# Two operations of the expert weights' rounding moved to GpSimd, and the context's keys and values started earlier

## The chip, the cores and the metric

The kernel runs on one core of a Trainium2 chip. The metric is the device time of one execution in microseconds, as the median of the runs; lower is better.

## The reference

Eight blocks of a transformer, each added to `x` (8 x 128 x 256, f32). The change lies in the second block, a mixture of experts, and in a piece of the seventh block that is computed beside it:

```python
x = x + _L0_xattn_ref(_layernorm(x), ctx_2048, ctx_2048)
x = x + _L0_ffn_ref(_layernorm(x), L0_ffn_gate_w, L0_ffn_w13, L0_ffn_w2, ...)
...
def mxfp8_qdq(x):                      # blocks of 32 along the last axis
    amax = jnp.max(jnp.abs(xb), axis=-1, keepdims=True)
    exp = jnp.floor(jnp.log2(jnp.where(amax > 0, amax, 1.0)))
    scale = jnp.exp2(jnp.clip(exp - E4M3_MAX_POW2, -127.0, 127.0))
    q = jnp.clip(xb / scale, -E4M3_MAX, E4M3_MAX).astype(jnp.float8_e4m3fn)
    return (q.astype(x.dtype) * scale).reshape(shp)
...
scores = jax.nn.sigmoid(xf @ gate_w.T)        # 8 experts, the best 2 of scores + bias
xq = mxfp8_qdq(routed)                        # tokens times their score
w13q, w2q = mxfp8_qdq(w13), mxfp8_qdq(w2)     # the experts' weights
h = silu(xq @ w13q_1) * (xq @ w13q_3)
out = mxfp8_qdq(h) @ w2q + shared expert
...
k = (inputs_kv @ Wk)   # L3 attention: keys and values of the context,
v = (inputs_kv @ Wv)   # which depend on no earlier block
```

## The kernel before

The stages run one after the other, with a barrier of all engines between them. Each stage is a block of five programs, one for each engine, that meet by semaphores; each program is executed in the order in which it is written. The first stage (`stage_l0_xattn`) is the first attention, with nothing on SP. The second (`stage_l0_ffn`) is the expert block. Its order on the engines, up to the first up projection:

- **SP** issues the loads of the gate and the shared expert, then of `wk` and `wv` (L535, 2 MB each), then for each of 24 pairs of weight tiles (`PAIRS`, 16 of `w13` and 8 of `w2`) the rows `wrow` (L542, two buffers) and, three pairs behind, the stores of the finished keys and values (L548, L552).
- **GpSimd** makes masks `diag` (L580, identity times routing mask, two operations of 128 x 1024 for each sequence): four sequences at once, the other four later, as the masks are used up.
- **VectorE** normalises (L228 to L238), copies the transposed tokens (L593), routes (L600 to L615), finishes the shared expert (L623, L627), rounds the tokens of three sequences (`quantise_tokens`, L635 and `mx_round`), then rounds the weights, pair by pair (`prep`, `mx_round`). `mx_round` is eleven operations on a 128 x 512 tile: mask of the exponents (L207, `magic`), maximum of each block of 32 (L208), five small ones on 128 x 16 (L209 to L214), the scale operation (L215), the addition of a large number and its subtraction (L217, L218), which round to the grid, and the upper and the lower cap (L219, L221). `order.step` makes the engine wait for the operation's own end before the next.
- **TensorE** transposes the tokens (L738), makes the gate's logits (L745), the shared expert (L753, L761), turns the tokens of the first sequence (`turn_tokens`, L774) and then, for each pair, transposes the rounded weights into `psW` (L788) and makes the units of keys and values that belong to the pair (`unit`, L796 for keys, L801 for values: 64 units of two products of 128 x 512, 2 or 3 a pair). Behind the last unit come the up projections (L819) of the first sequence.
- **ScalarE** copies what TensorE made: `xm` (L694), `wT` (L701), `held` (L707).

A pair's semaphores are `row_loaded` (SP to VectorE), `wq_ready` (rounded; to TensorE, and to SP for the next load), `turned` and `wT_ready`.

## Time and profile before

| what | us |
|---|---|
| median of 3 runs | 1996.21 (1995.42 to 1996.57) |
| the profiled execution, its own time | 2003.36 |
| its span, first to last instruction | 2001.6 |
| TensorE busy | 1613.5 (81%) |
| VectorE busy | 1387.7 (69%) |
| ScalarE busy | 823.7 (41%) |
| GpSimd busy | 605.3 (30%) |

The span is what the trace covers; the execution's own time is 1.8 us longer. The expert block lies at 80.5 to 396 us. "PEclk" in the views is the clock that was granted to TensorE, as a share of 2.4 GHz. PE is TensorE, PEld its weight loads, DVE VectorE, ACT ScalarE, POOL GpSimd, SP the engine that only issues DMAs here.

### The profile page before, as it was taken

What the parts mean: (1) busy time and instruction counts of PE and PEld (TensorE: products, weight loads), DVE (VectorE), ACT (ScalarE), POOL (GpSimd) and SP (SyncE); (2) the same over time, 40 slices, a digit from 0 to 9 for tenths busy, and PEclk for the clock granted to TensorE, in tenths of its full rate; (3) what the DMA queues carried; (4) which work ended last, traced back from release to release, by engine and by line L of the source; (5) the groups of instructions that cost most, each with busy time, mean ns of one, the idle gap of its engine ahead of it and who ended that gap; (6) DMA issues with size and microseconds to landing.
All of it is one profiled execution on the core that took longest, in us unless ns stands there. A gap on an engine that the chain in (4) does not pass through costs nothing. (4 is left out here: it accounts for less than half of the span.)

```text
span 2001.6 us, 30042 instructions
## 1 busy us (share of the span) xinstructions
PE 1613.5 (81%) x9326; PEld 1135.7 (57%) x9326; DVE 1387.7 (69%) x3901; ACT 823.7 (41%) x2380; POOL 605.3 (30%) x739
## 2 busy tenths in 40 slices
PE   3559998879353788988889699999987999799883
PEld 2424434356122466666666488788774555688872
DVE  6679969678796688888888634676555333468875
ACT  1113444457332466666667433333331222244451
POOL 0020003067401777777777430111122000321000
PEclk7579999969665999999999899999997999899996
DMA  1305620010382900000000150000035222522200
GB/s 63 110 1 158 194 101 1 13 67 1 9 156 75 343 1 1 2 1 1 1 1 2 31 173 1 26 12 12 11 144 149 75 87 74 179 103 101 69 25 11
DMA packets 103590, 129.34 MB, mean 65 GB/s; under 512 B 14160, under 2 KB 89136, under 8 KB 99984
## 3 DMA queue, kind: packets, MB, share of 16 engines
q1 hardware_dynamic: 94448, 112.39, 17.7%
q0 software_dynamic: 8992, 15.08, 3.6%
q8 instruction: 78, 1.28, 0.3%
q14 instruction: 72, 0.59, 0.1%
HBM read 85.75 MB, written 46.94 MB: 66 GB/s over the span
## 5 line engine op out<-in xcount | busy, mean ns | idle before, releaser
L2326 PE MATMUL l2fa_psQ<-l2fa_xT,l2f_home 128*128 128x128 f32 x1024 | 124.9, 283 | 0.7 <-DMA l2f_home<-in_L2f_kvT 0.7
L2326 PEld LDWEIGHTS l2fa_psQ<-l2fa_xT,l2f_home 128*128 128x128 f32 x1024 | 121.8, 199 | 3.1 <-issue 1.6
L580 POOL TENSOR_TENSOR l0f_diag<-g_identb,l0f_mask 128x1024 bf16<-128x1024 bf16 x16 | 32.0, 2025 | 227.7 <-PE l0f_psA L836 208.8
L2817 ACT ACTIVATE l2x_probs<-l2x_psS,l2x_nmax 128x128 f32<-128x128 f32 x256 | 90.7, 371 | 10.2 <-DVE l2x_nmax L2731 10.0
L2601 POOL TENSOR_TENSOR l2x_probs<-l2x_probs,l2x_rtotal 128x512 f32<-128x512 f32 x64 | 66.8, 1043 | 90.2 <-DVE l2x_rtotal L2737 90.2
L3102 POOL TENSOR_TENSOR route_rrms<-route_vrms,g_minus_half 128x1 f32<-128x1 f32 x8 | 5.7, 707 | 270.6 <-DVE route_vrms L3124 270.6
L2612 POOL TENSOR_TENSOR l2x_vsm<-l2x_vraw,l2x_smooth_row 128x512 f32<-128x512 f32 x64 | 84.7, 1345 | 3.7 <-ACT l2x_vraw L2851 3.4
L3687 POOL DMA_INDIRECT routed_rows<-rows,route_slot_of x32 | 31.2, 975 | 175.7 <-DMA rows<-moe_yg 167.0
L3511 DVE COPY moe_xgT<-moe_psX 128x256 f32<-128x256 f32 x47 | 20.0, 425 | 91.1 <-PE moe_psX L3617 91.1
L2962 PEld LDWEIGHTS l2x_psS<-l2x_kT,l2x_qT 128*128 128x128 f32 x512 | 66.8, 192 | 22.3 <-issue 17.9
L1427 ACT ACTIVATE l2fa_probs<-l2fa_psS,l2fa_bias 128x128 f32<-128x128 f32 x128 | 45.2, 365 | 76.6 <-DVE l2fa_bias L1411 76.6
L1040 ACT ACTIVATE l1a_probs<-l1a_psS,l1a_nmax 128x256 f32<-128x256 f32 x128 | 58.9, 472 | 42.1 <-PE l1a_psT L1068 29.7
L819 PE MATMUL l0f_psH<-l0f_wT,l0f_xm 128*128 128x512 bf16 x256 | 68.0, 390 | 9.7 <-DVE l0f_h L660 9.0
L960 POOL TENSOR_TENSOR l1a_probs<-l1a_probs,l1a_rtotal 128x512 f32<-128x512 f32 x64 | 65.2, 1040 | 32.7 <-DVE l1a_rtotal L998 32.7
L2860 ACT COPY l2x_pT<-l2x_psT 128x512 f32<-128x512 f32 x64 | 37.5, 586 | 90.2 <-PE l2x_psT L2970 90.2
L3610 PE MATMUL moe_psG<-l2f_home,moe_xgT 128*128 x188 | 68.0, 484 | 5.1 <-issue 1.5
L2978 PE MATMUL l2x_psO<-l2x_pT,l2x_vsm 128*128 128x128 f32 x512 | 70.5, 283 | 0.0
L2363 PE MATMUL l2fa_psY<-l2fa_wo,l2fa_oT 128*128 128x256 f32 x256 | 62.9, 390 | 8.5 <-DVE l2fa_oT L2233 8.5
L2962 PE MATMUL l2x_psS<-l2x_kT,l2x_qT 128*128 128x128 f32 x512 | 67.8, 276 | 1.8 <-ACT l2x_probs L2817 1.7
L2363 PE MATMUL l3a_psY<-l2f_home,l3a_oT 128*128 128x256 f32 x256 | 62.9, 390 | 7.4 <-DVE l3a_oT L2233 7.1
L2326 PE MATMUL l3a_psQ<-l3a_xT,routed_wq 128*128 128x128 f32 x512 | 65.2, 282 | 2.9 <-ACT l3a_qT L2283 2.3
L2583 POOL TENSOR_TENSOR l2x_qrstd<-l2x_qve,g_minus_half 128x4 f32<-128x4 f32 x64 | 65.3, 1020 | 5.3
(571 smaller groups left out, 4690.2 us busy)
## 6 DMA issues: line engine op xcount, KB each, us to landing
rows<-l2x_zero SPq DMA_DIRECT2D x1, 18304.0 KB, 59.9
kT_ctx<-l0f_held SPq DMA_DIRECT2D x32, 256.0 KB, 3.5
v_ctx<-l0f_held SPq DMA_DIRECT2D x32, 256.0 KB, 3.7
l3a_kT<-kT_ctx SPq DMA_DIRECT2D x8, 1024.0 KB, 5.3
l3a_v<-v_ctx SPq DMA_DIRECT2D x8, 1024.0 KB, 5.6
l0f_wrow<-in_L_ffn_w SPq DMA_DIRECT2D x24, 256.0 KB, 3.0
moe_xg<-rows SPq DMA_DIRECT2D x47, 128.0 KB, 2.0
rows<-moe_yg SPq DMA_DIRECT2D x47, 128.0 KB, 1.7
```

The source lines that it names most:

```text
L819: last = nc.tensor.matmul(psH[:, k, :], xm[b % 2][:, k, c, e, :], wT[:, 2 * e:2 * e + 2, c, :], start=(e == 0 and c == 0), stop=(e == E0 - ...
L960: nc.gpsimd.tensor_tensor(probs[:, u, j, :, :], probs[:, u, j, :, :], rtotal[:, u, j, :].unsqueeze(2).to_broadcast([P, 2, D]), ALU.mult)\
L1040: last = nc.scalar.activation(probs[:, u, j, m, :], psS[2 * u + j][:, m, :], ACT.Exp, bias=nmax[:, u, j, m:m + 1], scale=1.0, accum_out=to ...
L2326: last = nc.tensor.matmul(psQ[bank][:, j, :], w[:, c, h * HD:(h + 1) * HD], xT[u][:, c, :], start=(c == 0), stop=(c == KC - 1))
L2363: last = nc.tensor.matmul(psY[:, :], oT[:, i % 2, j, :], wo[:, 4 * i + j, :], start=(i == 0 and j == 0), stop=(i == QUADS - 1 and j == 3))
L2583: ins = nc.gpsimd.tensor_tensor(qrstd[:, t % 2, :], qve[:, :], G.minus_half[:, 0:4], ALU.pow)
L2601: nc.gpsimd.tensor_tensor(probs[:, n % 2, :, :], probs[:, n % 2, :, :], rtotal[:, n % 2, :].unsqueeze(2).to_broadcast([P, 4, P]), ALU.mult)\
L2612: nc.gpsimd.tensor_tensor(vsm[:, j % 3, 4 * g:4 * g + 4, :].rearrange("p (g r) d -> p g r d", r=2), vraw[:, j % 2, 2 * g:2 * g + 2, :].uns ...
L2817: last = nc.scalar.activation(probs[:, n % 2, j, :], psS[:, j, :], ACT.Exp, bias=nmax[:, n % 2, j:j + 1], scale=1.0, accum_out=total[:, n ...
L2962: last = nc.tensor.matmul(psS[:, j, :], qT[:, n % 4, j, :], kT[:, n // 2 % 2, 2 * (n % 2) + j // 2, :], start=True, stop=True)
L2978: last = nc.tensor.matmul(psO[:, j, :], vsm[:, n // 2 % 3, 4 * (n % 2) + j, :], pT[:, n % 2, j, :], start=True, stop=True)
L3610: last = nc.tensor.matmul(psG[m % 3][:, 0:2 * I2], x, w, start=(c == 0), stop=(c == KC - 1))
```

## The change

1. `mx_round` is cut into `mx_level` (up to the scale operation), the two operations of the grid, and `mx_cap`. Tokens and hidden rows still go through all of it on VectorE. For the weights GpSimd does the addition and the subtraction (`snap`), and VectorE works on the level of pair n + 1 before the caps of pair n. There are two sets of `magic`, `sum`, `grid`, `top` and `bottom`, and three buffers of rows instead of two; a row is loaded again once the addition has read it.
2. The level of pair 0 is made ahead of the routing. The tokens of the first three sequences are rounded behind pairs 6, 12 and 18; the first sequence's are turned behind pair 20.
3. `wk` and `wv` are allocated outside the two stages and loaded by SP during the first attention.
4. TensorE makes five units before it transposes the tokens; the other 59 are spread over the pairs, and those of a pair come before its transposes instead of behind them.

The core of the diff:

```diff
+def mx_level(nc, order, m, src):
 
     dve = nc.vector
-    n, nb = m.n, m.nb
-    blocks = lambda ap: ap.rearrange("p (n k) -> p n k", k=BLOCK)
-    spread = lambda ap: ap.unsqueeze(2).to_broadcast([P, nb, BLOCK])
     order.mark(dve.tensor_scalar(m.magic[:, :].bitcast(I32), src.bitcast(I32), EXPONENT, None, ALU.bitwise_and))
-    order.step(dve.tensor_reduce(m.amax[:, :], blocks(src), AX.X, ALU.max, apply_absolute_value=True))
+    order.step(dve.tensor_reduce(m.amax[:, :], blocks_of(src), AX.X, ALU.max, apply_absolute_value=True))
     order.step(dve.tensor_scalar(m.exp[:, :].bitcast(I32), m.amax[:, :].bitcast(I32), EXPONENT, None,
                                  ALU.bitwise_and))
 
     dve.tensor_scalar(m.top[:, :], m.exp[:, :], 2.0 ** -119, 1.75, ALU.max, ALU.mult)
     dve.tensor_scalar(m.bottom[:, :], m.exp[:, :], 2.0 ** -119, -1.75, ALU.max, ALU.mult)
     order.step(dve.tensor_scalar(m.least[:, :], m.exp[:, :], 2.0 ** -119, GRID * 2.0 ** -14, ALU.max, ALU.mult))
-    order.step(dve.scalar_tensor_tensor(out=blocks(m.magic[:, :]), in0=blocks(m.magic[:, :]), scalar=GRID,
-                                        in1=spread(m.least[:, :]), op0=ALU.mult, op1=ALU.max))
-    order.step(dve.tensor_tensor(m.sum[:, :], src, m.magic[:, :], ALU.add))
-    order.step(dve.tensor_tensor(m.grid[:, :], m.sum[:, :], m.magic[:, :], ALU.subtract))
-    order.step(dve.tensor_tensor(blocks(m.grid[:, :]), blocks(m.grid[:, :]), spread(m.top[:, :]), ALU.min))
-
-    return dve.tensor_tensor(blocks(dst), blocks(m.grid[:, :]), spread(m.bottom[:, :]), ALU.max)
+    return dve.scalar_tensor_tensor(out=blocks_of(m.magic[:, :]), in0=blocks_of(m.magic[:, :]), scalar=GRID,
+                                    in1=spread_of(m, m.least[:, :]), op0=ALU.mult, op1=ALU.max)
...
+def mx_cap(nc, order, m, dst):
+    order.step(nc.vector.tensor_tensor(blocks_of(m.grid[:, :]), blocks_of(m.grid[:, :]), spread_of(m, m.top[:, :]), ALU.min))
+    return nc.vector.tensor_tensor(blocks_of(dst), blocks_of(m.grid[:, :]), spread_of(m, m.bottom[:, :]), ALU.max)
+
+
+def mx_round(nc, order, m, src, dst):
+    order.step(mx_level(nc, order, m, src))
+    order.step(nc.vector.tensor_tensor(m.sum[:, :], src, m.magic[:, :], ALU.add))
+    order.step(nc.vector.tensor_tensor(m.grid[:, :], m.sum[:, :], m.magic[:, :], ALU.subtract))
+    return mx_cap(nc, order, m, dst)
...
+class ContextWeights:
+
+
+    def __init__(self, nc, ctx, G):
+        T = Pool(nc, ctx, "l0k")
+        self.wk, self.wv = T.sb("wk", [P, KC, NH * HD]), T.sb("wv", [P, KC, NH * HD])
+        self.wk_loaded, self.wv_loaded = G.sem("wk_loaded"), G.sem("wv_loaded")
+
+    def load(self, sp, A):
+        sp.dma_start(self.wk[:, :, :], A["L3_xattn_Wk"].rearrange("(c p) o -> p c o", p=P)).then_inc(self.wk_loaded, 16)
+        sp.dma_start(self.wv[:, :, :], A["L3_xattn_Wv"].rearrange("(c p) o -> p c o", p=P)).then_inc(self.wv_loaded, 16)
+
+
+def stages_l0(nc, G, A):
+    with ExitStack() as ctx:
+        C = ContextWeights(nc, ctx, G)
+        stage_l0_xattn(nc, G, A, C)
+        stage_l0_ffn(nc, G, A, C)
...
+            @block.sync
+            def _(sp):
+                C.load(sp, A)
...
-        wrow = [T.sb(f"wrow{u}", [P, 2, D]) for u in range(2)]
+        ROWS = 3
+        wrow = [T.sb(f"wrow{u}", [P, 2, D]) for u in range(ROWS)]
         wq = [T.sb(f"wq{u}", [P, 2, D], BF16) for u in range(2)]
         wT = T.sb("wT", [P, PAIRS, KC, 2 * P], BF16)
         mx = Mx(T, "mx", 512)
+        wmx = [mx, Mx(T, "mx1", 512, mx)]
...
-        units_of = lambda n: range(n * UNITS // PAIRS, (n + 1) * UNITS // PAIRS)
-        PREP_STEPS = MX_STEPS
+        EARLY, LATE = 5, UNITS - 5
+        units_of = lambda n: range(EARLY + n * LATE // PAIRS, EARLY + (n + 1) * LATE // PAIRS)
+        TOKENS_AFTER, TURN_AFTER = {6: 0, 12: 1, 18: 2}, 20
...
-                for w, name in ((wk, "L3_xattn_Wk"), (wv, "L3_xattn_Wv")):
-                    sp.dma_start(w[:, :, :], A[name].rearrange("(c p) o -> p c o", p=P)).then_inc(kv_loaded, 16)
...
-                    wait(sp, wq_ready, n - 1)
+                    wait(sp, summed, n - ROWS + 1)
                     src = w13[n] if n < PAIRS13 else w2[n - PAIRS13]
-                    sp.dma_start(wrow[n % 2][:, :, :], src).then_inc(row_loaded[n % 2], 16)
+                    sp.dma_start(wrow[n % ROWS][:, :, :], src).then_inc(row_loaded[n % ROWS], 16)
 
                 def store(m):
                     sp.wait_ge(kv_copied, m + 1)
@@ -554,6 +591,9 @@
 
                 for n in range(PAIRS):
                     rows(n)
+                    if n == 3:
+                        for m in range(EARLY):
+                            store(m)
...
+                def snap(n):
+                    m = wmx[n % 2]
+                    pool.wait_ge(leveled, n + 1)
+                    nc.gpsimd.tensor_tensor(m.sum[:, :], wrow[n % ROWS][:, :, :].rearrange("p r d -> p (r d)"), m.magic[:, :],
+                                            ALU.add).then_inc(summed, 1)
+                    pool.wait_ge(summed, n + 1)
+                    wait(pool, wq_ready, n - 1)
+                    nc.gpsimd.tensor_tensor(m.grid[:, :], m.sum[:, :], m.magic[:, :], ALU.subtract).then_inc(snapped, 1)
+
                 for b in range(B):
+                    if b == 4:
+                        for n in range(PAIRS):
+                            snap(n)
...
+                prep = Order(dve, prep_order)
+
+                def level(n):
+                    dve.wait_ge(row_loaded[n % ROWS], 16 * (n // ROWS) + 16)
+                    mx_level(nc, prep, wmx[n % 2], wrow[n % ROWS][:, :, :].rearrange("p r d -> p (r d)")).then_inc(leveled, 1)
+
+                def cap(n):
+                    dve.wait_ge(snapped, n + 1)
+                    wait(dve, turned, n - 1)
+                    mx_cap(nc, prep, wmx[n % 2], wq[n % 2][:, :, :].rearrange("p r d -> p (r d)")).then_inc(wq_ready, 1)
+
+                level(0)
...
-                for b in range(3):
-                    quantise_tokens(b)
-
-                def prep(n, u):
-                    o = Order(dve, prep_order, n * PREP_STEPS)
-                    dve.wait_ge(row_loaded[u], 8 * (n - u) + 16)
-                    wait(dve, turned, n - 1)
-                    mx_round(nc, o, mx, wrow[u][:, :, :].rearrange("p r d -> p (r d)"),
-                             wq[u][:, :, :].rearrange("p r d -> p (r d)")).then_inc(wq_ready, 1)
-                    assert o.n == PREP_STEPS, o.n
-                in_pairs(dve, PAIRS, prep)
+                for n in range(PAIRS):
+                    if n + 1 < PAIRS:
+                        level(n + 1)
+                    cap(n)
+                    if n in TOKENS_AFTER:
+                        quantise_tokens(TOKENS_AFTER[n])
...
+                for m in range(EARLY):
+                    copy_unit(m)
...
-                copy_tokens(0)
...
                 for n in range(PAIRS):
-                    prep(n, n % 2)
                     for m in units_of(n):
                         copy_unit(m)
+                    prep(n, n % 2)
+                    if n == TURN_AFTER:
+                        copy_tokens(0)
...
+                pe.wait_ge(C.wk_loaded, 16)
+                for m in range(EARLY):
+                    unit(m)
+                pe.wait_ge(kv_copied, EARLY)
...
-                pe.wait_ge(shared_added, B)
-                for n in range(XM):
-                    turn_tokens(0, n)
-                pe.wait_ge(xm_ready, XM)
...
-                pe.wait_ge(kv_loaded, 32)
                 for n in range(PAIRS):
-                    prep(n, n % 2)
                     for m in units_of(n):
                         unit(m)
+                    prep(n, n % 2)
+                    if n == TURN_AFTER:
+                        pe.wait_ge(kv_copied, units_of(n).stop)
+                        for i in range(XM):
+                            turn_tokens(0, i)
+                        pe.wait_ge(xm_ready, XM)
```

How the order of VectorE's instructions changes for one pair (`prep_order`, `snapped`, `turned` and `row_loaded` are the semaphores waited for). Before, the second half of a pair and the start of the next:

```order
L215 SCALAR_TENSOR_TENSOR l0f_mx_magic<-l0f_mx_magic,l0f_mx_least 128x512 [waits l0f_prep_order]
L217 TENSOR_TENSOR l0f_mx_sum<-l0f_wrow,l0f_mx_magic 128x512 [waits l0f_prep_order]
L218 TENSOR_TENSOR l0f_mx_grid<-l0f_mx_sum,l0f_mx_magic 128x512 [waits l0f_prep_order]
L219 TENSOR_TENSOR l0f_mx_grid<-l0f_mx_grid,l0f_mx_top 128x512 [waits l0f_prep_order]
L221 TENSOR_TENSOR l0f_wq<-l0f_mx_grid,l0f_mx_bottom 128x512 [waits l0f_prep_order]
```

After, on VectorE:

```order
L219 SCALAR_TENSOR_TENSOR l0f_mx_magic<-l0f_mx_magic,l0f_mx_least 128x512 [waits l0f_prep_order]
L224 TENSOR_TENSOR l0f_mx_grid<-l0f_mx_grid,l0f_mx_top 128x512 [waits l0f_turned,l0f_snapped]
L225 TENSOR_TENSOR l0f_wq<-l0f_mx_grid,l0f_mx_bottom 128x512 [waits l0f_prep_order]
L211 TENSOR_SCALAR l0f_mx_magic<-l0f_wrow 128x512 [waits l0f_row_loaded2]
L212 TENSOR_REDUCE l0f_mx_amax<-l0f_wrow 128x16
L213 TENSOR_SCALAR l0f_mx_exp<-l0f_mx_amax 128x16 [waits l0f_prep_order]
```

and on GpSimd, behind the first masks, pairs 0 to 2 (`leveled` is set by the scale operation):

```order
L632 TENSOR_TENSOR l0f_diag<-g_identb,l0f_mask 128x1024 x7
L620 TENSOR_TENSOR l0f_mx_sum<-l0f_wrow,l0f_mx_magic 128x512 [waits l0f_leveled]
L624 TENSOR_TENSOR l0f_mx_grid<-l0f_mx_sum,l0f_mx_magic 128x512 [waits l0f_summed]
L620 TENSOR_TENSOR l0f_mx_sum<-l0f_wrow,l0f_mx_magic 128x512 [waits l0f_leveled]
L624 TENSOR_TENSOR l0f_mx_grid<-l0f_mx_sum,l0f_mx_magic 128x512 [waits l0f_summed]
L620 TENSOR_TENSOR l0f_mx_sum<-l0f_wrow,l0f_mx_magic 128x512 [waits l0f_leveled]
L624 TENSOR_TENSOR l0f_mx_grid<-l0f_mx_sum,l0f_mx_magic 128x512 [waits l0f_wq_ready,l0f_summed]
```

The addition and the subtraction have left VectorE's row of five; the scale operation's own end is no longer waited for by the operation behind it, and the caps are those of the pair before.

TensorE at the end of the loop, before (the last pair's transposes, its three units, the first up projection):

```order
L788 MATMUL l0f_psW<-g_identb,l0f_wq 128x128 x3
L801 MATMUL l0f_psA<-l0f_wv,g_ctxT 128x512 [waits l0f_kv_copied]
L801 MATMUL l0f_psA<-l0f_wv,g_ctxT 128x512
L801 MATMUL l0f_psA<-l0f_wv,g_ctxT 128x512 [waits l0f_kv_copied]
L801 MATMUL l0f_psA<-l0f_wv,g_ctxT 128x512
L801 MATMUL l0f_psA<-l0f_wv,g_ctxT 128x512 [waits l0f_kv_copied]
L801 MATMUL l0f_psA<-l0f_wv,g_ctxT 128x512
L819 MATMUL l0f_psH<-l0f_wT,l0f_xm 128x512 [waits l0f_xm_ready,l0f_wT_ready,l0f_kv_copied]
```

After, from the transposes of pair 20 on:

```order
L864 MATMUL l0f_psW<-g_identb,l0f_wq 128x128 x3
L855 MATMUL l0f_psA<-l0f_diag,l0f_zq 128x512 [waits l0f_diag_ready,l0f_zq_ready,l0f_kv_copied]
L855 MATMUL l0f_psA<-l0f_diag,l0f_zq 128x512 x3
L855 MATMUL l0f_psA<-l0f_diag,l0f_zq 128x512 [waits l0f_xm_ready] x4
L807 MATMUL l0f_psA<-l0k_wv,g_ctxT 128x512 [waits l0f_kv_copied,l0f_xm_ready]
```

The turning of the tokens stands between pair 20 and the eight units of pairs 21 to 23; the units of a pair stand ahead of its transposes, and nothing stands between the last transposes and the up projection (L885).

## Rows read from the trace of the kernel before

**Rows 1.** Busy us by stretch; behind the engines the granted clock, DMA share, GB/s.

```profile
core 0: us, PE busy (x) PEld busy (x) DVE busy (x) ACT busy (x) POOL busy (x), PEclk, DMA share, GB/s
80.00:88.00 8.00, 0.00 (x0) 0.00 (x0) 5.59 (x24) 0.00 (x0) 2.09 (x3) 0.50 0.57 146
100.00:104.00 4.00, 4.00 (x6) 1.86 (x7) 3.36 (x7) 1.51 (x2) 0.00 (x0) 0.50 0.03 12
104.00:110.00 6.00, 5.09 (x12) 1.91 (x10) 5.83 (x8) 1.19 (x2) 5.16 (x3) 1.00 0.00 0
131.00:154.00 23.00, 3.92 (x12) 1.24 (x13) 21.94 (x53) 4.01 (x8) 0.00 (x0) 0.58 0.00 0
170.00:271.50 101.50, 97.81 (x293) 43.59 (x292) 96.75 (x218) 41.38 (x73) 0.00 (x0) 1.00 0.62 189
```

**Rows 2.** Timeline, VectorE, a pair's ends: start us, duration us, engine, line, out<-in.

```profile
256.10 0.42 DVE L207 TENSOR_SCALAR l0f_mx_magic<-l0f_wrow 128x512 int32<-128x512 int32 x1
...
259.90 0.69 DVE L219 TENSOR_TENSOR l0f_mx_grid<-l0f_mx_grid,l0f_mx_top 128x512 bf16<-128x512 bf16 x1
260.62 0.69 DVE L221 TENSOR_TENSOR l0f_wq<-l0f_mx_grid,l0f_mx_bottom 128x512 bf16<-128x512 bf16 x1
261.23 0.42 DVE L207 TENSOR_SCALAR l0f_mx_magic<-l0f_wrow 128x512 int32<-128x512 int32 x1
```

**Rows 3.** Timeline, end of the loop; a unit is four records of L801.

```profile
262.20 3.65 PE L801 MATMUL l0f_psA<-l0f_wv,g_ctxT 128*128 128x512 f32 x8
...
266.74 5.37 PE L801 MATMUL l0f_psA<-l0f_wv,g_ctxT 128*128 128x512 f32 x12
...
270.89 0.69 DVE L221 TENSOR_TENSOR l0f_wq<-l0f_mx_grid,l0f_mx_bottom 128x512 bf16<-128x512 bf16 x1
...
272.17 5.37 PE L801 MATMUL l0f_psA<-l0f_wv,g_ctxT 128*128 128x512 f32 x12
...
278.21 0.60 PE L819 MATMUL l0f_psH<-l0f_wT,l0f_xm 128*128 128x512 bf16 x2 [0.68 <-ACT l0f_held L707]
```

**Rows 4.** Instructions of one line, GpSimd: duration ns min/median/max, first and last start.

```profile
L2601 POOL TENSOR_TENSOR l2x_probs<-l2x_probs,l2x_rtotal x64: 1030/1039/1097, 680.1 to 1132.8; 128x512 f32<-128x512 f32 x64
...
L2562 POOL TENSOR_TENSOR l2x_scaled<-l2x_xn,cw_in_row x16: 1256/1267/1276, 640.9 to 1013.7; 128x512 bf16<-128x512 f32 x16
```

**Rows 5.** Timeline, VectorE and GpSimd at the second and third later masks.

```profile
300.32 3.94 POOL L580 TENSOR_TENSOR l0f_diag<-g_identb,l0f_mask 128x1024 bf16<-128x1024 bf16 x2 [180.56 <-PE l0f_psA L836]
...
302.42 0.67 DVE L208 TENSOR_REDUCE l0f_mx_amax<-l0f_h 128x16 f32<-128x512 f32 x1
...
303.13 1.16 DVE L209 TENSOR_SCALAR l0f_mx_exp<-l0f_mx_amax 128x16 int32<-128x16 int32 x1
...
312.98 0.69 DVE L219 TENSOR_TENSOR l0f_mx_grid<-l0f_mx_grid,l0f_mx_top 128x512 bf16<-128x512 bf16 x1
...
313.07 4.66 POOL L580 TENSOR_TENSOR l0f_diag<-g_identb,l0f_mask 128x1024 bf16<-128x1024 bf16 x2 [8.81 <-PE l0f_psA L836]
...
313.71 2.27 DVE L221 TENSOR_TENSOR l0f_zq<-l0f_mx_grid,l0f_mx_bottom 128x512 bf16<-128x512 bf16 x1
```

**Rows 6.** Instructions of one line, start of the third stage, at 403 to 410.

```profile
L984 DVE TENSOR_SCALAR l1a_q<-g_x,l1a_mv,l1a_rstd x8: 396/481/4014, 403.3 to 409.7; 128x256 f32<-128x256 f32 x8
...
L952 POOL TENSOR_SCALAR l1a_ks<-g_ctx,l1a_parity x16: 478/479/504, 403.2 to 483.8; 128x256 f32<-128x256 f32 x16
```

**Rows 7.** Timeline, ahead of the loop: two token roundings' starts and the turned tokens' casts.

```profile
130.94 0.61 DVE L635 TENSOR_SCALAR l0f_z<-l0f_xf,l0f_wslot 128x256 f32<-128x256 f32 x2
...
136.72 0.61 DVE L635 TENSOR_SCALAR l0f_z<-l0f_xf,l0f_wslot 128x256 f32<-128x256 f32 x2
...
137.53 4.01 ACT L694 CAST l0f_xm<-l0f_psA 128x512 bf16<-128x512 f32 x8 [14.92 <-PE l0f_psA L774]
```

**Rows 8.** Timeline, start of the expert block up to the gate's scores.

```profile
88.67 3.67 PE L738 MATMUL l0f_psA<-g_ident,l0f_xf 128*128 128x128 f32 x16 [9.36 <-DVE l0f_xf L238]
...
93.22 6.96 PE L745 MATMUL l0f_psO<-l0f_gateT,l0f_xfT 128*128 128x8 f32 x32 [0.87 <-DVE l0f_xfT L593]
...
100.47 0.20 DVE L600 TENSOR_SCALAR l0f_scores<-l0f_scores 128x64 f32<-128x64 f32 x1 [7.40 <-ACT l0f_scores L682]
```

More of the change, by code:

```diff
@@ L25 @@
 KC = D // P
-STAGES = range(4)
+STAGES = range(3)
 NH = 16
@@ L449, in route, with stage_l0_ffn @@
     order.step(dve.tensor_reduce(rank[:, :, :], gt[:, :, :, :], AX.X, ALU.add))
-def stage_l0_ffn(nc, G, A):
+def stage_l0_ffn(nc, G, A, C):
     with ExitStack() as ctx:
@@ L733, in _, with unit @@
             def _(pe):
+                def unit(m):
+                    wait(pe, kv_copied, m - 3)
+                    for c in range(KC):
+                        if m < UNITS // 2:
+                            h, half = divmod(m, 2)
+                            last = nc.tensor.matmul(psA[m % 4][:, :], wk[:, c, h * HD:(h + 1) * HD],
+                                                    G.ctxT[:, c, 4 * half:4 * half + 4, :].rearrange("p b t -> p (b t)"),
+                                                    start=(c == 0), stop=(c == KC - 1))
+                        else:
+                            if m == UNITS // 2 and c == 0:
+                                pe.wait_ge(C.wv_loaded, 16)
+                            b, i = divmod(m - UNITS // 2, NH // 4)
+                            last = nc.tensor.matmul(psA[m % 4][:, :], G.ctxT[:, c, b, :], wv[:, c, 512 * i:512 * (i + 1)],
+                                                    start=(c == 0), stop=(c == KC - 1))
+                    last.then_inc(kv_done, 1)
+                pe.wait_ge(C.wk_loaded, 16)
+                for m in range(EARLY):
+                    unit(m)
+                pe.wait_ge(kv_copied, EARLY)
                 pe.wait_ge(T.ln_ready, 1)
```

48 lines of the change are left out of this document (21 added, 27 removed).

## The prediction

> **What bounds the kernel now.** I read the stages by their windows first, then one pair of weight tiles on VectorE, then TensorE at the end of that loop, and last GpSimd's prices and its neighbours. The change touches one stretch, from the end of the first attention at 80.5 us to the first up projection of the experts at 278.2 us. What follows is in the same order in both kernels, so the shift of the first up projection is the shift of the end.
>
> In 170 to 271.5 VectorE was busy 96.75 of 101.50 us and TensorE 97.81 [rows 1]. Both are nearly full, so both have to be counted. One pair on VectorE goes from the masking at 256.10 to the next one at 261.23, 5.13 us; an operation of 512 elements that the next one waits for takes 0.72 (259.90 to 260.62), the last one 0.61 (to 261.23) [rows 2]. On TensorE two units of keys and values took 3.65 and three 5.37, so one unit is 1.72 us; from the three units of 266.74 to the next ones at 272.17 it is 5.43, so the four transposes between add 0.27 [rows 3]. 64 units in 24 pairs are 2.67 a pair, 4.59 us, with the transposes 4.86. VectorE's 5.13 is the longer one, TensorE follows closely. After the last rounding (270.89, 0.69) TensorE still had three units to make, and the up projection began at 278.21, 6.6 us behind it [rows 3]. Ahead of the loop TensorE had little to do: busy 3.92 of 23 us in 131 to 154 and nothing in 80 to 88 [rows 1].
>
> **VectorE's pair.** Two operations leave, 2 x 0.72 = 1.45, and the scale operation is no longer waited for by the next one, 0.12 (0.72 less 0.61). Left to itself a pair would be 5.13 - 1.57 = 3.56 us: 2.33 for the level part, 1.33 for the two caps, less 0.1 by which neighbours overlap.
>
> **GpSimd's price.** The add has two full f32 inputs, and so has the subtract. The rows for 512 elements are 1039 ns where the second input is four numbers spread out, and 1267 with two f32 inputs, there with the bf16 output of the subtract [rows 4]. I take 1.27 for both and keep 1.04 as the low end. [...]
>
> **Whether the two engines run side by side.** This decides the case. At 313.07 GpSimd began two masks of 1024 elements while VectorE was in the operation of 312.98; the next VectorE operation, the same upper and lower cap as in the weights' rounding, took 2.27 us instead of 0.69, and the two masks took 4.66 instead of 2 x 1.9. At 303.13 an operation on 16 elements took 1.16 instead of 0.17 beside the masks of 300.32; the reduction of 302.42 took its usual 0.67 [rows 5]. So operations with two SBUF inputs and tensor-scalar operations wait for GpSimd's, each in turn, and the reduction does not. Of the nine VectorE operations of a pair only the reduction is free. The mask of 1.9 cost the cap 1.58, which is its duration less 0.3; an add of 1.27 then costs the lower cap 0.96.
>
> Now in order. The scale operation ends; the upper cap follows at once, before GpSimd has the signal; the add takes the port when that cap ends, as the mask did after 312.98; the lower cap waits 0.96. The subtract wants the port while the lower cap holds it. Behind that cap VectorE's masking is queued without a wait between them. If the subtract, which waits already, goes first, the masking waits about 1.06 more. The nearest rows are the normalisation at 403: VectorE's scaling, 396 ns alone, took a median of 481 beside GpSimd's, back to back on both sides, and GpSimd's stayed at 479, at most 504 [rows 6]. GpSimd lost no turn there, so I let it go first. The pair is 3.56 + 0.96 + 1.06 = **5.58 us**, 0.45 more than before; from the end of a scale operation to that of the lower cap it is 0.60 + 0.72 + 0.96 = 2.28. Its ends: 5.1 with GpSimd at 1.04, and 6.1 if both operations block for their whole 1.27.
>
> The Trainium skill (SBUF, State Buffer, section Who interferes with whom) says that issue order, not the shape of the operation, decides who blocks. No row here shows that hand-over for these very operations; by it the subtract, issued first, goes first, and the sum is the one above.
>
> **The loop and its tail.** VectorE was free for the first token rounding at 130.94; one such rounding takes 5.78 (to 136.72) [rows 7]. The level of pair 0 moves to where VectorE waits for the gate scores, 7.40 us with nothing in it [rows 8], and its GpSimd part behind the fourth mask; both cost nothing. The three token roundings move into the loop, same work. The weights of pair 20 are then ready at 130.94 + 2.33 + 20 x 5.58 + 2.28 + 3 x 5.78 = 264.5 us. From there TensorE is the late one: the transposes 0.4; turning the tokens, which stood at 137 to 141.5 with 4.01 us of casts, 4.8 with the wait for the casts [rows 7]; then the units of pairs 21 to 23, 3 + 2 + 3 = 8, 13.8; three groups of transposes 0.8; the last copies 1.2. That is 21.0, and the up projection begins at 285.5, against 278.2: **+7.3**. The three units behind the last rounding are gone, but the turning of the tokens, done before at a time when TensorE stood idle, now lies in the tail; without it there TensorE would be some 3.5 us earlier. DMAs: the same 24 row loads with one buffer more, and the same 64 stores. The row load waits for the add instead of the lower cap of the pair before, which comes later by nothing that the third buffer does not cover. The 4 MB of projections load during the first attention, where neither SP nor the DMA queues do anything; cost nothing, and if it were late, only the five early units would wait. VectorE's pairs are written out now instead of standing in a loop of two pairs a turn; TensorE's always were and ran without a gap in 170 to 271.5 [rows 1]: nothing.
>
> **The early units.** TensorE starts five units at 80.6. The granted clock was 0.50 there and stayed so in 100 to 104, the first 4 us of dense matmuls, and was 1.00 in 104 to 110 [rows 1]. With 4 us at half (1.2 units) and the rest at 1.72 the five end at 91.2, their last copy at 91.9, and the transposes, at 88.67 before [rows 8], begin 3.2 us later. At full clock they are no longer the bound of the four copies behind them: 1.3 us back. The gate matmuls took 6.96 at half clock [rows 8]; if the clock stays up they take some 3.5, if it falls behind the first ones 6 or so. I take **+1.0** for the start (ends: -1.6, and +9.8 less what follows if all five ran at half).
>
> **Sum.** +7.3 + 1.0 = +8.3 us on the profiled execution (span 2001.6 to 2009.9, its own time 2003.36 to 2011.7). That execution lies 7 us above the median of the three runs; the shift goes onto the median: 1996.2 + 8.3 = **2004.5 us**.
>
> **Rivals.** *VectorE keeps the port between two operations queued without a wait.* Then the masking goes before the subtract, which runs beside the reduction; only 0.35 of the second wait is left and the pair is 4.87. Twenty pairs are 14.2 us less, the token roundings give back 1.8: 8.3 - 12.4 = -4.1, **1992.1 us**, faster. For it: the masking is back to back with the cap. Against it: [rows 6]. It decides as soon as the pair is below 5.2 us, since then the loop gains more than start and tail cost. *The port hardly matters for these operations*: the pair is 3.56, the weights of pair 20 come at 223, where TensorE has just made its units (130.6 + 51 x 1.72 + 21 x 0.27 = 224), and the up projection begins at 245: -32, **1964 us**. Against it stand all of [rows 5]; for it only that those masks have 1024 elements. *The start costs more*, because the clock stays at 0.50 through most of the early units, or falls again before the shared experts: +4 to +6 more, **2010 us**. That GpSimd does not do the two operations can't be: the order of its instructions shows them.
>
> **Numbers.** Forecast 0.60, VectorE keeps the port 0.20, port hardly matters 0.06, dear start 0.14. The range 1989 to 2012 leaves out the third, the lower part of the second and the top of the last. A difference below 0.2% (4 us) can't be told from none. Faster 0.06 + 0.11 of the second + 0.03 of the forecast (GpSimd at 1.04) = 0.20; within 0.09 + 0.05 = 0.14; slower 0.66.
>
> **What would show it.** In the changed profile: a VectorE pair of 5.6 us with the lower cap at 1.6 to 1.7 and the masking at 1.4 to 1.5 instead of 0.69 and 0.42; GpSimd's add and subtract near 1.65, since each waits for a cap; TensorE idle about 0.9 us before each group of transposes, and no VectorE wait for GpSimd's signal. The first up projection near 286.5. I am wrong if the masking keeps its 0.42 (then the first rival), if the caps do too (the second), or if TensorE shows no idle time in the loop.

## The result and the profile after

| | before, us | changed, us | ratio |
|---|---|---|---|
| first comparison, median of 5 and 5 runs | 1996.57 (1995.42 to 2004.1) | 2007.94 (2007.48 to 2014.3) | 1.0058 [1.0037, 1.0079] |
| second, on another chip, 25 and 10 runs | 2001.02 (1991.34 to 2006.78) | 2007.32 (2005.3 to 2012.79) | 1.0039 [1.0020, 1.0058] |

The changed kernel is slower, by 11.4 us in the first comparison and 6.3 in the second. The forecast was 2004.5 us, and slower with a chance of 0.66.

The stretches of the changed kernel that answer to [rows 1] (same columns):

```profile
core 0: us, PE busy (x) PEld busy (x) DVE busy (x) ACT busy (x) POOL busy (x), PEclk, DMA share, GB/s
80.00:88.00 8.00, 7.40 (x13) 3.29 (x14) 5.57 (x24) 1.32 (x3) 2.09 (x3) 0.73 0.67 185
131.00:154.00 23.00, 18.04 (x56) 7.72 (x55) 22.15 (x38) 7.48 (x13) 12.89 (x8) 1.00 0.46 138
170.00:259.00 89.00, 64.47 (x179) 27.74 (x176) 86.39 (x156) 26.04 (x46) 41.49 (x27) 0.90 0.42 138
259.00:264.00 5.00, 4.60 (x9) 2.20 (x10) 4.86 (x10) 1.02 (x2) 2.75 (x2) 0.50 0.19 52
268.00:289.00 21.00, 18.15 (x50) 7.69 (x50) 9.29 (x14) 9.41 (x18) 6.48 (x4) 0.92 0.24 93
```

VectorE still has no room in the loop (86.39 of 89 us); TensorE now has some (64.47, where [rows 1] had 97.81 of 101.5). The sign of this kernel is in the fourth row: at 259 TensorE works at a granted clock of 0.50, its lower level (1.2 GHz), having idled; in the kernel before the clock was 1.00 all along in 170 to 271.5.

One pair on VectorE, which answers to [rows 2], and GpSimd's part of it (start us, duration us):

```profile
228.35 0.69 DVE L219 SCALAR_TENSOR_TENSOR l0f_mx_magic<-l0f_mx_magic,l0f_mx_least 128x512 f32<-128x512 f32 x1
228.96 0.69 DVE L224 TENSOR_TENSOR l0f_mx_grid<-l0f_mx_grid,l0f_mx_top 128x512 bf16<-128x512 bf16 x1
229.68 1.64 DVE L225 TENSOR_TENSOR l0f_wq<-l0f_mx_grid,l0f_mx_bottom 128x512 bf16<-128x512 bf16 x1
231.24 1.49 DVE L211 TENSOR_SCALAR l0f_mx_magic<-l0f_wrow 128x512 int32<-128x512 int32 x1
232.65 0.67 DVE L212 TENSOR_REDUCE l0f_mx_amax<-l0f_wrow 128x16 f32<-128x512 f32 x1
...
236.81 1.49 DVE L211 TENSOR_SCALAR l0f_mx_magic<-l0f_wrow 128x512 int32<-128x512 int32 x1
```

```profile
229.12 1.65 POOL L620 TENSOR_TENSOR l0f_mx_sum<-l0f_wrow,l0f_mx_magic 128x512 f32<-128x512 f32 x1 [2.26 <-DVE l0f_mx_magic L219]
230.84 1.60 POOL L624 TENSOR_TENSOR l0f_mx_grid<-l0f_mx_sum,l0f_mx_magic 128x512 bf16<-128x512 f32 x1
```

From masking to masking it is 236.81 - 231.24 = 5.57 us. The lower cap takes 1.64 instead of 0.69, the masking 1.49 instead of 0.42, the reduction keeps its 0.67, and the add and the subtract read as 1.65 and 1.60, where the first ones, at 119.29 and 120.64 beside a nearly idle VectorE, took 1.27 and 1.26. From 132 to 280 us the trace has no wait of VectorE for GpSimd: what GpSimd costs is in the durations.

TensorE in a usual pair, behind the last token rounding, and at the end of the loop, which answers to [rows 3]:

```profile
231.60 3.65 PE L807 MATMUL l0f_psA<-l0k_wv,g_ctxT 128*128 128x512 f32 x8
236.95 0.40 PE L864 MATMUL l0f_psW<-g_identb,l0f_wq 128*128 128x128 bf16 x4 [1.69 <-DVE l0f_wq L225]
237.18 5.37 PE L807 MATMUL l0f_psA<-l0k_wv,g_ctxT 128*128 128x512 f32 x12
...
259.40 0.61 PE L864 MATMUL l0f_psW<-g_identb,l0f_wq 128*128 128x128 bf16 x4 [5.70 <-DVE l0f_wq L225]
259.80 6.34 PE L807 MATMUL l0f_psA<-l0k_wv,g_ctxT 128*128 128x512 f32 x8
...
265.98 0.39 PE L864 MATMUL l0f_psW<-g_identb,l0f_wq 128*128 128x128 bf16 x4
267.04 2.70 PE L855 MATMUL l0f_psA<-l0f_diag,l0f_zq 128*128 128x512 bf16 x7 [0.68 <-ACT l0f_held L743]
271.31 7.11 PE L807 MATMUL l0f_psA<-l0k_wv,g_ctxT 128*128 128x512 f32 x12 [1.57 <-ACT l0f_xm L760]
278.26 0.39 PE L864 MATMUL l0f_psW<-g_identb,l0f_wq 128*128 128x128 bf16 x4
278.49 3.65 PE L807 MATMUL l0f_psA<-l0k_wv,g_ctxT 128*128 128x512 f32 x8
281.97 0.39 PE L864 MATMUL l0f_psW<-g_identb,l0f_wq 128*128 128x128 bf16 x4
282.20 5.37 PE L807 MATMUL l0f_psA<-l0k_wv,g_ctxT 128*128 128x512 f32 x12
...
288.78 1.46 PE L885 MATMUL l0f_psH<-l0f_wT,l0f_xm 128*128 128x512 bf16 x5 [0.99 <-ACT l0f_held L743]
```

The up projection begins at 288.78, against 278.21 before: +10.57. Two units (x8) took 6.34 us behind the idle stretch of 5.70, and 3.65 in pairs without a token rounding. Three (x12) took 7.11 behind the turning of the tokens, and 5.37 elsewhere, behind a wait of 1.69 too. The first two token roundings show the same: behind idle stretches of 7.41 and 5.69 us three units took 7.99 (at 181.44) and two took 5.46 (at 220.61), but there the waits of the pairs that follow take the loss up.

**How far a time can be read here.** The profiled execution of the kernel before lies 7 us above its median, that of the changed kernel on its median; the changed one is 10.3 us behind when the third stage begins (407.28 against 397.01) and 4.5 us behind at the end (spans 2006.1 and 2001.6). On the chips of the experiments, runs of the kernel before alone spread over 12 to 17 us. Two executions of the changed kernel differed by 6.0 us in what follows the first up projection (span 2006.1 with it at 288.78, span 2010.5 with it at 287.20), and over the fourteen traces of this case that part took from 1716.6 to 1724.5 us. So the theories are told apart by the start of the first up projection, which repeated within 1.6 us in those two executions; times stand beside it. Where a run below has one execution, its time can't be told from this spread.

### The profile page after: what moved, and what is told of

It reads as the page before. It is cut to its first block and busy times, and to the rows that moved or that the text cites. A ratio compares the mean times of both kernels' runs of the same rounds, so it can differ in the third digit from the quotient of the medians.

```text
span 2006.1 us, 29797 instructions
## 1 busy us (share of the span) xinstructions
PE 1606.0 (80%) x9245; PEld 1128.8 (56%) x9326; DVE 1397.2 (70%) x3853; ACT 824.2 (41%) x2380; POOL 683.2 (34%) x787
## 5 line engine op out<-in xcount | busy, mean ns | idle before, releaser
L2883 ACT ACTIVATE l2x_probs<-l2x_psS,l2x_nmax 128x128 f32<-128x128 f32 x256 | 90.7, 371 | 10.7 <-DVE l2x_nmax L2797 10.3
L743 ACT COPY l0f_held<-l0f_psA 128x512 f32<-128x512 f32 x64 | 37.4, 585 | 96.3 <-PE l0f_psA L800 53.8
L885 PE MATMUL l0f_psH<-l0f_wT,l0f_xm 128*128 128x512 bf16 x256 | 66.9, 384 | 10.5 <-DVE l0f_h L719 9.0
```

Of the source, the lines that this page charges most:

```text
L885: last = nc.tensor.matmul(psH[:, k, :], xm[b % 2][:, k, c, e, :], wT[:, 2 * e:2 * e + 2, c, :], start=(e == 0 and c == 0), stop=(e == E0 - ...
L2883: last = nc.scalar.activation(probs[:, n % 2, j, :], psS[:, j, :], ACT.Exp, bias=nmax[:, n % 2, j:j + 1], scale=1.0, accum_out=total[:, n ...
```

## The experiments

My theory was the prediction's: VectorE's operations wait for GpSimd's in turn, 0.96 and 1.06 us a pair, and TensorE's tail (the time from the weights of pair 20 to the first up projection) adds the rest. The rivals are that the early units or the new waits cost the time, or that the tail is bound by something else.

**1. Add and subtract back on VectorE.**

```diff
-                    wait(sp, summed, n - ROWS + 1)
+                    wait(sp, wq_ready, n - ROWS + 1)
...
-                        for n in range(PAIRS):
-                            snap(n)
...
-                    dve.wait_ge(snapped, n + 1)
+                    m = wmx[n % 2]
+                    dve.wait_ge(leveled, n + 1)
+                    prep.step(nc.vector.tensor_tensor(m.sum[:, :], wrow[n % ROWS][:, :, :].rearrange("p r d -> p (r d)"),
+                                                      m.magic[:, :], ALU.add))
+                    prep.step(nc.vector.tensor_tensor(m.grid[:, :], m.sum[:, :], m.magic[:, :], ALU.subtract))
```

A row's next load then waits for the pair's lower cap, since no `summed` is left.

> The changed kernel with the add and the subtract of each pair back on VectorE, behind the masking; everything else of the change (split rounding, context's keys and values first, early load) stays. Theory 1 (GpSimd's two operations and the handovers with them cost VectorE 5.58 - 5.1 = about 0.45 us a pair, and the early units next to nothing): a pair takes 5.1 to 5.2 us again, wq of pair 20 is ready near 255.5, the first up projection starts at 278 to 281 instead of 288.8, and the time is 1997 to 2000, close to the kernel before. Rival (the early units and the extra waits cost the time, GpSimd does not): the pair is free of GpSimd but the time stays within 2 us of 2008.

The first up projection comes at 277.82, 10.96 us earlier than in the profile above. A pair takes 5.01 us, under the forecast, since the scale operation is not waited for either. The time is 2002.0 us, the kernel before on this chip 2002.48 (ratio 1.0002 [0.9984, 1.0019]). So the whole shift goes with GpSimd's two operations, what their pace does to TensorE included; the early units, the order and the waits that stay cost nothing together (277.82 against 278.21 in the kernel before).

**2. The same operations on GpSimd, but small.** They round 16 of the 512 columns and leave out the others, so most of the rounded weights is a constant. The addition is cut in the same way.

```diff
-                    nc.gpsimd.tensor_tensor(m.grid[:, :], m.sum[:, :], m.magic[:, :], ALU.subtract).then_inc(snapped, 1)
+                    nc.gpsimd.tensor_tensor(m.grid[:, 0:16], m.sum[:, 0:16], m.magic[:, 0:16], ALU.subtract).then_inc(snapped, 1)
...
```

> The changed kernel with GpSimd's add and subtract on 16 of the 512 columns only (the rest of the rounded weights is a constant zero, so the output is not the reference's); all waits, the order and the number of instructions stay. Theory 1 (the price is the time that GpSimd's 512 columns take beside VectorE on the memory's side, 1.06 + 0.96 us a pair): VectorE's pair falls to 3.6 to 4.0 us of its own work, TensorE with 4.5 us a pair becomes the pace, the first up projection starts at 247 to 252, time 1965 to 1972. Rival (the handover by semaphores costs it: VectorE waits for the engine, not for the memory): the pair stays above 5.2 us and the time above 2000.

A pair takes 3.58 us, the first up projection comes at 247.81, the time is 1969.29 (before 2002.48; 0.9843 [0.9801, 0.9886]). VectorE and GpSimd in one pair:

```profile
202.59 0.69 DVE L224 TENSOR_TENSOR l0f_mx_grid<-l0f_mx_grid,l0f_mx_top 128x512 bf16<-128x512 bf16 x1
203.31 0.69 DVE L225 TENSOR_TENSOR l0f_wq<-l0f_mx_grid,l0f_mx_bottom 128x512 bf16<-128x512 bf16 x1
203.92 0.44 DVE L211 TENSOR_SCALAR l0f_mx_magic<-l0f_wrow 128x512 int32<-128x512 int32 x1
```

```profile
202.76 0.60 POOL L622 TENSOR_TENSOR l0f_mx_sum<-l0f_wrow,l0f_mx_magic 128x16 f32<-128x16 f32 x1 [2.25 <-DVE l0f_mx_magic L219]
203.44 0.65 POOL L626 TENSOR_TENSOR l0f_mx_grid<-l0f_mx_sum,l0f_mx_magic 128x16 bf16<-128x16 f32 x1
```

The same signals are sent and waited for, and VectorE's operations run as if alone. So the price is the work of GpSimd's 512 columns, not the handover by semaphores. The prediction's figure for a pair left to itself, 3.56, holds, and the up projection comes at the early end of the 247 to 252 expected.

**3. One of the two.** The add is on VectorE, the subtract on GpSimd.

> The changed kernel with the add back on VectorE (behind the masking) and the subtract alone on GpSimd. Theory (each GpSimd operation of 1.27 us costs the VectorE operation it runs beside about 1 us, and saves VectorE 0.69 us): VectorE has 3.56 + 0.69 = 4.25 us of its own and one operation held for about 1 us, 5.2 to 5.3 us a pair, between the 5.01 us with none on GpSimd and the 5.58 us with both; the weights of pair 20 near 258 to 260, the first up projection at 281 to 284. Rival (the two held operations hinder each other, one alone is cheap): a pair at 4.6 us or less, the first up projection below 275.

A pair takes 5.23 us, the weights of pair 20 are ready at 258.9, and the first up projection comes at 282.62. The time of the one execution is 2007.36 (before, one too, 1995.13), which does not show those 6.2 us.

```profile
235.13 0.68 DVE L224 TENSOR_TENSOR l0f_mx_grid<-l0f_mx_grid,l0f_mx_top 128x512 bf16<-128x512 bf16 x1
235.84 1.64 DVE L225 TENSOR_TENSOR l0f_wq<-l0f_mx_grid,l0f_mx_bottom 128x512 bf16<-128x512 bf16 x1
237.41 0.41 DVE L211 TENSOR_SCALAR l0f_mx_magic<-l0f_wrow 128x512 int32<-128x512 int32 x1
```

One operation on GpSimd lengthens one on VectorE by 0.95 us, and the masking behind is free again at 0.41. The costs add: 5.01 with none, 5.23 with one, 5.58 with two. Moving an operation saves VectorE 0.69 to 0.72 us and costs it 0.95 to 1.07.

**4. The turning of the first tokens behind pair 7**, `TURN_AFTER` 20 to 7.

> The changed kernel with the turning of the first tokens (a block of TensorE's work and a wait for the last token rounding) placed behind pair 7 instead of pair 20; the token roundings stay where they are (behind pairs 6, 12, 18), so this turning now waits for the third of them. If the tail of 24 us between pair 20 and the first up projection is TensorE's work that piled up while it idled at half clock, its place matters: with the pair still at 5.58 us the first up projection should come between 281 and 283, or, where the early wait for the third rounding (ready near 255) blocks TensorE's in-order queue, later than 288.8: 11 pairs of transposes and units at 4.5 us would then stand behind it and VectorE would be held by its two buffers. Theory (the tail is what is late): 2001 to 2002. Rival (blocked queue): 2030 or more, by up to 11 x 4.5 us less what VectorE would have taken anyway.

A pair takes 5.58 us, the weights of pair 20 are ready at 265.1, and the first up projection comes at 283.12, 5.66 us earlier and just past the 281 to 283 expected. The time is 2004.14 us, before 2002.48 (1.0009 [0.9986, 1.0032]). My fear in the expectation was unfounded: the turning began at 181.64, right behind the transposes of pair 7. It needs the first rounding alone, so TensorE's queue was not blocked.

**5. The three token roundings early, and the turning behind them.**

```diff
-TOKENS_AFTER, TURN_AFTER = {6: 0, 12: 1, 18: 2}, 20
+TOKENS_AFTER, TURN_AFTER = {0: 0, 2: 1, 4: 2}, 6
```

> The changed kernel with the three token roundings behind pairs 0, 2 and 4 instead of 6, 12 and 18, and their turning behind pair 6 instead of pair 20; no instruction is added or dropped. Theory (VectorE's loop sets the pace at 5.58 us a pair, its own total is unchanged, and what it moves is only TensorE's tail, which stands at 23.8 us in the changed kernel and holds 4.8 us of turning and about 3 us lost to a clock at half after idle gaps): the last pair's weights are ready near 280 as before, the first up projection starts at 281 to 283 instead of 288.8, the time is 2000 to 2002. Rival (the tail is bound by something else, a load or ScalarE's casts): the up projection stays within 2 us of 288.8, time 2006 to 2010.

The first up projection comes at 282.79, 5.99 us earlier, with pairs of 5.58. The time is 2001.76 us, before 2002.48 (1.0004 [0.9984, 1.0023]). The tail is TensorE's own work: with the turning out of it the up projection comes 4.3 us behind the last pair's weights. The up projection is still 4.6 us behind that of the kernel before and the time is not, which is within the spread told of above.

**6. The third token rounding alone, two pairs earlier**, `18: 2` to `16: 2`; the turning stays behind pair 20.

> The changed kernel with the third token rounding behind pair 16 instead of pair 18; the turning stays behind pair 20, and no instruction is added or dropped. It tests the term that was mis-sized: TensorE came out of 5.7 us of idling behind the third rounding at a granted clock of 0.50 and made the two units at 259.80 in 6.34 us instead of 3.65, just ahead of the turning. Theory (these 2.7 us were lost in the tail because nothing behind them idles): with the third rounding two pairs earlier the idle stretch and the slow units lie before pair 18, the units of the pairs up to 20 catch up in the waits of 0.9 us a pair, and the tail from the weights of pair 20 to the first up projection is 20.5 to 21.5 us instead of 23.3 to 23.8; the weights of pair 20 stay at 264 to 265, the first up projection comes at 284.5 to 286.5 instead of 287.2 to 288.8. Rival (the tail was under-sized in its own work): it stays at 23 us or more.

The weights of pair 20 are ready at 264.7, the first up projection begins at 285.52: the tail is 20.8 us. The time of the one execution is 2010.55 (before 1996.76), above the changed kernel's medians, though the up projection is earlier. Its TensorE:

```profile
248.42 4.99 PE L807 MATMUL l0f_psA<-l0k_wv,g_ctxT 128*128 128x512 f32 x8
...
265.00 1.03 PE L855 MATMUL l0f_psA<-l0f_diag,l0f_zq 128*128 128x512 bf16 x4
...
269.75 5.42 PE L807 MATMUL l0f_psA<-l0k_wv,g_ctxT 128*128 128x512 f32 x12 [1.57 <-ACT l0f_xm L760]
...
285.52 0.59 PE L885 MATMUL l0f_psH<-l0f_wT,l0f_xm 128*128 128x512 bf16 x2 [0.98 <-ACT l0f_held L743]
```

and the granted clock there:

```profile
247.00:252.00 5.00, 3.98 (x10) 1.95 (x11) 4.86 (x10) 0.85 (x2) 2.66 (x3) 0.66 0.20 52
264.00:286.00 22.00, 18.08 (x59) 7.88 (x60) 12.97 (x21) 10.65 (x20) 8.24 (x6) 1.00 0.26 99
```

The instructions are the same, and the slow units now lie at 248, where pairs with room follow. In the tail the clock is at its full level throughout. The three units behind the turning take 5.42 instead of 7.11, behind the same wait of 1.57 for the casts: that wait alone does not slow them.

**7. Without the early units**, `EARLY` 5 to 0, all 64 units in the pairs.

> The changed kernel without its early units: all 64 units of context's keys and values are spread over the pairs, as before. Theory (the early five cost the start about 1 us or less and take their 8.6 us of TensorE out of a loop that VectorE paces, where 24 x 5.58 us have room for them): the masking of pair 1 at 130.3 to 131.2 instead of 131.6, a pair stays at 5.58 us, the first up projection at 288 to 290.5. Rival (the early units are worth their TensorE time): the first up projection at 292 or later. Second rival (they cost the start dear): the start 3 us or more earlier and the up projection below 286.

The masking of pair 1 comes at 129.25, earlier than in the changed kernel's two executions (131.64, 130.55), and the first up projection at 286.23, 1.0 to 2.6 us earlier. The time of the one execution is 2008.05 (before 1995.13). This lies between the theory and the second rival. From that masking to the up projection it is 156.98 us, against 157.14 and 156.65: at the pace of 5.58 the early units give nothing back in the loop. That they cost the start 1 to 2.4 us is not shown by one execution, since the start moves by as much by itself (run 10).

**8. The changed kernel again.**

> The changed kernel itself, unaltered, so that the runs beside it on this chip have it as a measure. Every theory: the first up projection at 288.8 within 0.3 us, a pair of 5.58 us. In time, 8 to 12 us above the kernel before on the same chip (where the 10.6 us of the first experts arrive at the end nearly whole); a rival, that the stages behind make up for it on other chips, gives under 4 us.

The first up projection comes at 287.20, not within 0.3 but 1.6 us earlier: 1.1 in the start (pair 1 at 130.55) and 0.5 in the tail (23.3 us), where the two units behind the idle stretch took 5.82 and the three behind the turning 7.11 again. The pair is 5.58 again. The time is 2007.32 us, 6.3 above before on this chip, between theory and rival.

**9. VectorE's rounding and early tokens together.** The edits of 1 and 5.

> The changed kernel with add and subtract on VectorE (pair 5.01 us measured) and the three token roundings behind pairs 0, 2 and 4, their turning behind pair 6. The two gains measured apart were 10.95 us (add and subtract back) and 5.99 us (tokens early). Theory, the two lie behind one another in the same wait of the first up projection: the weights of the last pair are ready at 269 to 270 as they were with the late tokens (269.2), and only the tail that was 8.6 us there shrinks to the 4.3 us of the early tokens: first up projection at 272.5 to 274.5, 4 to 5 us before the kernel before (278.2), time 3 to 6 us below it. Rival (the two gains add up): first up projection near 271.8 or earlier. Rival (the tail returns elsewhere in the expert loop): time within 1 us of before.

The weights of the last pair are ready at 269.7, the first up projection comes at 273.83, and the time is 1993.77 us against 2001.02 (0.9965 [0.9948, 0.9982]). The theory holds. The two gains don't add (14.95 us together, 10.96 and 5.99 apart), since both shorten the wait for the same instruction, and VectorE's own work is the floor.

**10. The kernel before, with GpSimd's masks later.**

```diff
     pool.wait_ge(masks_ready, TOP0)
+    pool.wait_ge(hid_ready, 2)
```

> The kernel before with one edit: GpSimd's eight mask products wait until the second hidden product is done. Theory (GpSimd's 14.9 us of mask products beside the route's small VectorE operations lengthen these, the same contention as in the changed kernel's pairs): the route is done 4 to 5 us earlier, the first token rounding begins at 126 to 127 instead of 130.94, the first up projection at 273 to 274.5 instead of 278.2, time 3 to 5 us below the kernel before. Rival (the route waits for ScalarE and TensorE, not for the memory): start and time unchanged within 1 us.

The gain is more than forecast: the first token rounding begins at 122.83 (before 130.94), and the first up projection at 270.48, 7.7 us earlier. The time is 1994.75 us against 2001.02 (0.9975 [0.9956, 0.9993]). VectorE's route in the kernel before, and with this edit:

```profile
104.79 2.06 DVE L609 TENSOR_TENSOR l0f_own<-l0f_mask,l0f_scores 128x64 f32<-128x64 f32 x2
106.89 0.29 DVE L611 TENSOR_REDUCE l0f_wslot<-l0f_own 128x16 f32<-128x128 f32 x1
107.21 1.44 DVE L612 TENSOR_TENSOR l0f_wsum<-l0f_wslot 128x8 f32<-128x8 f32 x1
108.69 1.82 DVE L613 TENSOR_SCALAR l0f_wsum<-l0f_wsum 128x8 f32<-128x8 f32 x1
...
112.41 1.29 DVE L623 TENSOR_TENSOR l0f_hidT<-l0f_hidT,l0f_psA 128x512 f32<-128x512 f32 x2
```

```profile
102.85 0.36 DVE L610 TENSOR_TENSOR l0f_own<-l0f_mask,l0f_scores 128x64 f32<-128x64 f32 x2
103.25 0.28 DVE L612 TENSOR_REDUCE l0f_wslot<-l0f_own 128x16 f32<-128x128 f32 x1
103.57 0.17 DVE L613 TENSOR_TENSOR l0f_wsum<-l0f_wslot 128x8 f32<-128x8 f32 x1
103.77 0.17 DVE L614 TENSOR_SCALAR l0f_wsum<-l0f_wsum 128x8 f32<-128x8 f32 x1
...
104.42 0.69 DVE L624 TENSOR_TENSOR l0f_hidT<-l0f_hidT,l0f_psA 128x512 f32<-128x512 f32 x1
```

An addition of 8 numbers a partition took 1.44 us beside a mask of 1024 and 0.17 alone; the reduction is untouched again. From the first of these to the hidden product it is 7.62 against 1.57 us, a gain of 6.05. Another 1.94 us were there before the masks began (102.85 against 104.79), and that part is not this edit's: the gate's scores came 1.94 us earlier (98.53 against 100.47), with a granted clock of 0.86 in 92 to 96 us, where the kernel before had 0.50.

**11. All together.** The edits of 1, 5 and 10, and pair 0 rounded whole in the wait for the scores.

```diff
                 level(0)
+                cap(0)
                 dve.wait_ge(scores_ready, 1)
...
-                    cap(n)
+                    if n > 0:
+                        cap(n)
```

> The kernel of the run with VectorE's rounding and early tokens, and two more edits: GpSimd's eight mask products wait until the hidden activations are multiplied (they ran beside VectorE's operations of the route from 104.4 us on and made these longer), and pair 0 is rounded whole in VectorE's wait for the scores instead of its front half alone. Theory: 4 to 5 us from the route (masking of pair 1 at 126 to 127 instead of 130.7) and 2.8 us from pair 0 (0.68 + 0.69 + 2 x 0.69), as VectorE sets the pace of the loop: first up projection at 265 to 267, 11 to 13 us before the kernel before; time 9 to 13 us below it. Rival (TensorE's units and transposes become the pace once VectorE starts earlier: 24 x 4.5 us from the first pair): first up projection not before 270.

The masking of pair 1 comes at 124.71 and the first up projection at 264.32, 13.9 us ahead of the kernel before, both more than forecast. The time is **1984.84 us** (1982.68 to 1987.68) against 2001.02, ratio 0.9921 [0.9891, 0.9951]. This version beats both kernels.

**12. All together without the early units.**

> The kernel of all_together without the early units (64 units spread over the pairs, as in the kernel before). Theory (the early five cost the start about 2 us, as the masking of pair 1 at 129.3 against 130.6 to 131.8 showed, and give nothing back while VectorE paces the loop): the first up projection 1 to 2 us earlier, at 262.3 to 263.3, the time within 2 us of all_together's 16 us below the kernel before. Rival (the loop is now so short that TensorE's 64 x 1.72 + 24 x 0.27 us = 117 us from the first pair at 125 become the bound, since VectorE's loop ends at 260 and TensorE idles through the first pairs): the first up projection at 266 or later.

The rival holds: the first up projection comes at 268.62, 4.3 us later than in run 11. The time is 1987.53 us against 1996.76 (0.9951 [0.9929, 0.9973]).

```profile
185.00:262.00 77.00, 77.00 (x232) 34.93 (x231) 70.54 (x159) 31.42 (x57) 0.00 (x0) 0.99 0.56 186
```

TensorE is busy in all of 185 to 262 (74.88 of 77 us in run 11), and it has three units left to make when the last pair's weights are ready at 262.3. VectorE, with 70.54, waits 3.3 us for loads of rows; SP issues these behind the stores of TensorE's units. From the masking of pair 1 to the up projection it is 143.13 us, against 139.61 in run 11. So once VectorE's side is short the early units are worth 3.5 us in the loop, where run 7 showed nothing; the other 0.8 lies in the start (125.49 against 124.71).

## Why the prediction was right, and where not

The forecast of the first up projection was 278.2 + 8.3 = 286.5; it came at 288.8 in the profile above and, in another execution, at 287.2. The shift was 10.6 us instead of 8.3, and the median 3.4 us above the forecast.

- **VectorE's pair, 5.58 forecast, 5.58 measured**, each part too: lower cap 1.64, masking 1.49, add and subtract near 1.65. Run 2 shows the 3.56 left to itself (3.58), run 3 that one GpSimd operation costs one held operation of 0.95, run 1 that all of the shift goes with these two. The choice on which the case hung, that the subtract goes ahead of the masking, came from [rows 6] and held: the masking took 1.48 or 1.49 in every pair but the first and the three behind a token rounding, where no cap stands right ahead of it. The rivals in which VectorE keeps its turn (pair 4.87) and in which the two hardly meet (3.56) are out, the second only because GpSimd's operations have 512 columns: with 16 it came true, at 247.8. TensorE's idle time was not the forecast 0.9 us ahead of each group of transposes but 1.69 ahead of every second one.
- **The start: +1.0 forecast, +0.70 measured** (131.64 against 130.94), and -0.4 in the second execution. The early units ended at 91.25, forecast 91.2, and the transposes began at 91.92, 3.25 us later, forecast 3.2:

```profile
80.60 10.65 PE L800 MATMUL l0f_psA<-g_ctxT,l0k_wk 128*128 128x512 f32 x20 [1.26 <-PEq L162]
91.92 1.97 PE L819 MATMUL l0f_psA<-g_ident,l0f_xf 128*128 128x128 f32 x16 [0.68 <-ACT l0f_held L743]
```

The rival of a dear start is out. That the sum came so near is in part luck. At the gate's scores the changed kernel was 0.41 us ahead (100.06 against 100.47); it lost 1.1 us behind them, in the shared expert, where the granted clock was 0.66 in 110 to 120 us against 0.83 in the kernel before and in the second execution. The prediction had only warned of that fall, in its last rival.

- **Weights of pair 20:** 264.5 + 1.0 of the start forecast, 264.94 measured.
- **The tail, 21.0 forecast, 23.84 measured: the term that was mis-sized.** The step had counted the eight units at 1.72 us each, the rate of the loop before, where the granted clock was 1.00 [rows 1]. I had written TensorE's new idle times down as a sign of the change, and had not asked what they do to its clock. Behind the third rounding TensorE idled 5.7 us in one piece and came out at 0.50; the two units ahead of the transposes of pair 20 took 6.34 instead of 3.65 and were still running when the weights of pair 20 were there (transposes at 265.98, not 264.94). The three units behind the turning took 7.11 instead of 5.37. That is 1.0 + 1.7 of the 2.8 us; the other steps are each within 0.2 of the forecast. Run 6 moves one rounding and has a tail of 20.8 us, near the forecast's 21.0, with the clock at 1.00.
- **What the median shows.** The shift of 10.6 us became 11.4 in the first comparison; in the second it was 9.0 us at the up projection of the profiled execution and 6.3 in the medians. Which of the later stages gives or takes these microseconds is open: they were not experimented on.

Nor did I see in [rows 5] and [rows 8] that the same contention already sat in the kernel before, in the route, where it costs 6 us at one place, more than half of the change's whole shift (run 10).

## What to carry to other kernels

Moving an operation from a full VectorE to GpSimd pays only if it lengthens what runs beside it on VectorE by less than it saves. Compare the duration saved (here 0.69 to 0.72) with GpSimd's own duration less what overlaps (here 0.95 to 1.07), read from one neighbouring pair of rows where the two engines already meet. Look for small VectorE operations that take 1 to 2 us instead of 0.2: here they stood beside a long GpSimd operation, and a later start of that one, which had slack, was the cheapest edit of all. Where a change gives TensorE idle time ahead of a stretch in which it is late, cost that stretch at the lower clock too, and place the idle time where room follows it.
